# Redone order of the first batch and of the end in a linear-attention kernel, with q's product on VectorE

## The reference

```python
xt = group_norm(x, 32 groups)                    # per batch, then tokens x channels
q, k, v = split(xt @ qkv_w.T + qkv_b)
q = relu(q); k = relu(k + pos_enc)               # 8 heads of 32 channels
z = 1 / (q . k.sum(tokens) + 1e-6)               # one number per token and head
kv = k^T v                                       # 32 x 32 per head
y = x + ((q @ kv) * z) @ proj_w.T + proj_b
```

## Time and profile before

| | |
|---|---|
| median of 3 runs | 2763.82 us (2762.53 to 2765.61) |
| profiled execution | 2772.32 us |
| its span | 2770.5 us |
| PE busy | 2625.4 us, 95% |
| DVE, ACT, POOL busy | 1610.3, 1664.1, 1929.7 us |
| HBM traffic | 519.25 MB read, 119.80 MB written |

### The profile page before, as it was taken

One profiled execution on the slowest core, in us unless ns is written; L12 is line 12 of the kernel. 1 busy time (PEld: TensorE's weight loads), 2 busy tenths in 40 slices (PEclk: granted clock), 3 DMA queues, 4 the chain that ended last, 5 costly groups with the idle time before them and its releaser, 6 DMA issues.

```text
span 2770.5 us, 45261 instructions
## 1 busy us (share of the span) xinstructions
PE 2625.4 (95%) x15812; PEld 2230.1 (80%) x15812; DVE 1610.3 (58%) x2525; ACT 1664.1 (60%) x2544; POOL 1929.7 (70%) x1192
## 2 busy tenths in 40 slices
PE   4779999999999999999999999999999999999985
PEld 3667878888887888878888887888888788888864
DVE  5555656656565566656666565565656566655443
ACT  3556656566565656666666665656656566665632
POOL 2436868687676877868687776867768686876842
PEclk9999999999999999999999999999999999999997
DMA  6446878788787887878788787868868787876756
GB/s 223 141 127 196 271 221 259 227 255 252 226 260 222 267 251 225 262 218 263 228 259 262 228 258 225 267 219 259 259 215 263 227 252 234 257 218 202 220 166 183
DMA packets 357471, 642.07 MB, mean 232 GB/s; under 512 B 34432, under 2 KB 55808, under 8 KB 357248
## 3 DMA queue, kind: packets, MB, share of 16 engines
q1 hardware_dynamic: 357248, 639.18, 74.3%
HBM read 519.25 MB, written 119.80 MB: 231 GB/s over the span
## 4 chain that ended last, share of the span: by engine, by line
PE 72%; DVE 10%; ACT 6%; issue 6%; POOL 3%; DMA 2%; SPq 1%; ACTq 0%; DVEq 0%; POOLq 0%
PE psK L514 17%; PE psX L536 15%; PE psX L567 15%; PE psG L526 10%; PE psG L528 5%; PE psT L505 5%; PE psX L553 3%; ACT xn L961 3%; DVE stats L767 2%; DVE psK L784 2%; DVE kk L789 2%; ACT xt L978 1%; POOL hl L1102 1%; POOL q L1120 1%; DVE zt L839 1%
## 5 line engine op out<-in xcount | busy, mean ns | idle before, releaser
L1116 POOL TENSOR_TENSOR kacc<-kacc,kt 128x512 f32<-128x512 f32 x368 | 478.4, 1300 | 380.5 <-ACT kt L990 378.0
L514 PE MATMUL psK<-wqk,hl 128*128 128x256 f32 x4608 | 651.3, 291 | 16.9 <-POOL hl L1102 16.9
L1102 POOL TENSOR_TENSOR hl<-xn,hl 128x512 fp32r<-128x512 f32 x384 | 497.6, 1318 | 243.2 <-ACT hl L973 243.2
L773 DVE TENSOR_TENSOR xt<-psT,xt 128x512 fp32r<-128x512 f32 x400 | 274.7, 687 | 626.9 <-ACT xt L978 626.8
L526 PE MATMUL psG<-kk,xt 128*128 128x512 f32 x1600 | 588.4, 401 | 21.4 <-DVE kk L789 21.4
L536 PE MATMUL psX<-hl,wqk 128*128 128x512 f32 x2304 | 600.4, 396 | 2.2 <-DVE xr L803 2.2
L514 PEld LDWEIGHTS psK<-wqk,hl 128*128 128x128 f32 x4608 | 580.5, 192 | 22.5 <-POOL hl L1102 22.5
L1120 POOL TENSOR_TENSOR q<-q,zb 128x1024 f32<-128x1024 f32 x192 | 461.5, 2404 | 158.3 <-DMA zb<-z_rows 158.3
L567 PE MATMUL psX<-uhl,mhl 128*128 128x512 f32 (+1 forms) x2364 | 557.7, 385 | 11.7 <-DVE uhl L899 11.7
L983 ACT ACTIVATE kk<-psK 128x512 fp32r<-128x512 f32 x400 | 239.8, 600 | 465.3 <-DVE psK L784 459.9
L567 PEld LDWEIGHTS psX<-uhl,mhl 128*128 128x128 f32 x2364 | 435.2, 189 | 103.0 <-DVE uhl L899 12.5
(11 more groups left out here) (112 smaller groups left out, 2354.8 us busy)
## 6 DMA issues: line engine op xcount, KB each, us to landing
zb<-z_rows SPq DMA_DIRECT2D x768, 128.0 KB, 4.4
posb<-pos_plus_bk SPq DMA_DIRECT2D x375, 256.0 KB, 5.4
xs<-in_x SPq DMA_DIRECT2D x184, 512.0 KB, 5.9
xa<-in_x SPq DMA_DIRECT2D x184, 512.0 KB, 6.0
xr<-in_x SPq DMA_DIRECT2D x184, 512.0 KB, 3.9
y<-xr SPq DMA_DIRECT2D x184, 512.0 KB, 6.7
z_rows<-zt SPq DMA_DIRECT2D x32, 256.0 KB, 5.4
posb<-in_pos SPq DMA_DIRECT2D x25, 256.0 KB, 2.8
```

The costliest lines, as they stand in the source:

```text
L514: last = mm(psK[:, par(n, h), i * C:(i + 1) * C], hl_of(t)[:, a, c, s:s + P], wqk[:, w, c, C:2 * C], start=(j == 0), stop=(j == len(terms) ...
L1102: g.tensor_tensor(hl_of(t)[:, 1, :, s], xn_of(n, t)[:, :, s], hl_of(t)[:, 0, :, s], ALU.subtract).then_inc(xl_ready, 1)
L1116: g.tensor_tensor(both, both, kt[:, par(n, h), :], ALU.add).then_inc(ks_done, 1)
```

## The change

Four things are edited.

1. `scale` moves from POOL to DVE in all steady steps, behind `key_low` of the first half; in step 2 of a batch it stands behind `key_add` of the second half and ahead of `m_low`.
2. The first batch gets its own ACT order (`first_step`), the position addition moves from DVE to POOL (`pos_add`), and the root of the first group norm comes ahead of the copy of the weights.
3. In step `LAST` ACT normalises block 0 of the next batch ahead of `key_high`.
4. The end is rewritten: queries and denominators come ahead of the outputs left over from the batch before (blocks 9 to 12), five places for `zb` instead of two, seven places for u instead of three, two pairs of PSUM banks instead of one for the copies of q, and DVE makes the low part of u ahead of the residual.

```diff
 # DVE, steady step
                 key_low(n, 2 * t)
+                if has_u(n, t) and t != 2:
+                    scale(*u_of(n, t))
...
                     if t == 2 and junction:
+
+                        scale(*u_of(n, t))
                         m_low(n - 1)
                     key_low(n, 2 * t + 1)
+            def scale(n, t):
+                dve.wait_ge(zb_landed[(NBLK * n + t) % 2], zb_no(n, t))
+                v.tensor_tensor(q_of(n, t), q_of(n, t), zb_of(n, t), ALU.mult).then_inc(u_ready, 1)
 # ACT, first batch
+            def first_step(t):
+
+                x_high_t(0, 2 * t)
+                key_high(0, 2 * t)
+                normalise(0, t + 1)
+                x_high_t(0, 2 * t + 1)
+                key_keep(0, 2 * t)
+                xn_high(0, t + 1)
+                if has_q(0, t):
+                    save_q(*q_at(0, t), 0, 2)
+                key_high(0, 2 * t + 1)
+                key_keep(0, 2 * t + 1)
+                if has_q(0, t):
+                    save_q(*q_at(0, t), 1, 0)
 # ACT, steady step
+                if t == LAST and n + 1 < B:
+
+                    normalise(n + 1, 0)
+                    xn_high(n + 1, 0)
                 key_high(n, 2 * t)
 # POOL
             def step(n, t):
-                if has_u(n, t):
-                    scale(*u_of(n, t))
+                if first(n) and t < LAST:
+                    pos_add(2 * t + 2)
+                    xn_low(0, t + 1)
+                    key_sum(0, 2 * t)
+                    if t < LAST - 1:
+                        pos_add(2 * t + 3)
+                    key_sum(0, 2 * t + 1)
+                    return
                 key_sum(n, 2 * t)
+            def scale_last(t):
+                pool.wait_ge(z_last[t % 5], 16 * HPC * (t // 5 + 1))
+                g.tensor_tensor(q_of(B - 1, t), q_of(B - 1, t), z_places[t % 5][:, :, 0:size(t)], ALU.mult).then_inc(u_ready, 1)
 # SP, the end
-            store_y(B - 2, LAST - 2)
-            load_last(4)
-            store_z(B - 1, 0)
-            load_zb(B - 1, 0)
-            load_zb(B - 1, 1)
+            store_z(B - 1, 0)
+            for t in range(5):
+                load_z_last(t)
+            store_y(B - 2, LAST - 3)
+            load_last(4)
+            store_y(B - 2, LAST - 2)
+            store_z(B - 1, 1)
+            load_z_last(5)
...
             for t in range(NBLK):
-                if t + 2 == 8:
-                    store_z(B - 1, 1)
-                if t + 2 < NBLK:
-                    load_zb(B - 1, t + 2)
                 store_last(t)
+                if t + 9 < NBLK:
+                    load_z_last(t + 9)
```

More of the change, by code:

```diff
@@ L91, in build @@
         nbias = sb("nbias", [P, CC])
[L93 to L96, removed]
+        banks8 = ps("banks8", [P, 8, BLK])
+        psG = banks8[:, 0:2, :]
+        psX = banks8[:, 2:5, :]
+        psT = banks8[:, 5, :]
+        psK = banks8[:, 6:8, :]
+        pairs = (psK, banks8[:, 4:6, :])
         zd = nc.dram_tensor("z_rows", (2, P, BLK), F32, kind="Internal").ap()
@@ L105, in build @@
         y_last = [sem(f"y_last{i}") for i in range(8)]
+        z_last = [sem(f"z_last{i}") for i in range(5)]
         x_first = [sem(f"x_first{i}") for i in range(4)]
@@ L421, in step @@
                     next_pos(n, 2 * t + 1)
-                if has_out(n, t):
+                if has_out(n, t) and (n, t) != (B - 1, LAST):
                     store_y(*out_of(n, t))
@@ L558, in output @@
                 k = size(t)
+                mw = mhl_last if n == B - 1 else mhl
                 pe.wait_ge(ul_ready, blk_no(n, t))
@@ L777, in key_add @@
                 s = pos_slot(n, h)
-                dve.wait_ge(pos_landed[s], pos_no(n, h))
                 if first(n):
-                    both = posb[:, s, :].rearrange("p (i n) -> p i n", i=TILES)
-                    v.tensor_tensor(both, both, bk_b[:], ALU.add).then_inc(pos_added, 1)
                     dve.wait_ge(pos_added, h + 1)
+                else:
+                    dve.wait_ge(pos_landed[s], pos_no(n, h))
                 dve.wait_ge(k_done, half_no(n, h))
@@ L992, in save_q, with save_from @@
             def save_q(n, t, m, bank):
+                save_from(n, t, m, psX[:, bank, 0:size(t)])
+            def save_from(n, t, m, src):
                 if m == 0:
-                    wait(act, ul_ready, blk_no(*q_gone(n, t)))
+                    if (n, t) == (B - 1, LAST - 1):
+                        act.wait_ge(kt_ready, NHB * B)
+                    else:
+                        wait(act, ul_ready, blk_no(*q_gone(n, t)))
                 act.wait_ge(q_done, two_no(n, t, m))
-                a(q_of(n, t)[:, m, :], psX[:, bank, 0:size(t)], ACT.Relu, bias=bq[:, m:m + 1]).then_inc(q_saved, 1)
+                a(q_of(n, t)[:, m, :], src, ACT.Relu, bias=bq[:, m:m + 1]).then_inc(q_saved, 1)
             def u_high(n, t, u, used):
@@ L1035, in step @@
                 key_keep(n, 2 * t)
-                nxt = (n, t + 1) if t < LAST else (n + 1, 0)
-                if nxt[0] < B:
-                    normalise(*nxt)
-                    xn_high(*nxt)
+                if (n, t) == (B - 1, LAST):
+                    return
+                if t < LAST:
+                    normalise(n, t + 1)
+                    xn_high(n, t + 1)
                 if t == 2 and not first(n):
@@ new lines, in u_last @@
+                    a(pairs[t % 2][:, :, 0:size(t)], q_of(n - 1, t), ACT.Copy)
+                    if t == 0:
+                        act.wait_ge(q_done, two_no(n - 1, q2, 1))
+                    elif t == 1:
+                        act.wait_ge(q_done, two_no(n - 1, q1, 1))
+                    elif t in (2, 3):
+                        act.wait_ge(g_done, NHB * n)
+                    elif t < 7:
+                        act.wait_ge(o_done, two_no(n - 2, t + 6, 1))
+                    else:
+                        act.wait_ge(o_done, two_no(n - 1, t - 7, 1))
@@ new lines, in u_last @@
+                    a(u_last_of[t % 7][:, 0, :, 0:size(t)], q_of(n - 1, t), ACT.Copy).then_inc(uh_ready, 1)
+                g_copy(n - 1)
+                save_q(n - 1, q2, 1, 0)
+                save_q(n - 1, q1, 0, 2)
+                z_plus(n - 1, 0, psK[:, 0, :])
+                save_from(n - 1, q1, 1, psK[:, 1, :])
+                act.wait_ge(q_done, two_no(n - 1, q0, 1))
+                for m in range(CC):
+                    save_from(n - 1, q0, m, psX[:, 2, m * HALF:(m + 1) * HALF])
@@ L1149, in _ @@
                 scale(B - 2, t)
-                u_low(B - 2, t, uhl)
+            for t, u in ((LAST - 2, hl[:, 0]), (LAST - 1, hl[:, 1]), (LAST, uhl)):
+                u_low(B - 2, t, u)
             for t in range(NBLK):
-                scale(B - 1, t)
+                scale_last(t)
 def kernel(**inputs):
```

167 lines of the change are left out of this document (111 added, 56 removed).

## The result

The changed kernel takes 2673.56 us (median of 4 runs, 2670.30 to 2675.03), the kernel before 2763.18 on the same chip (4 runs, 2760.95 to 2765.61): ratio 0.9674, 95% interval 0.9657 to 0.9691. The forecast was 2681, the range 2652 to 2716. The medians moved by 89.6 us, the forecast said 83.

A forecast was written before the change was run, and what follows sets the result against it. PE was taken as full in the steady part, with loops of waits in the first batch and at the end. Savings of 44 + 6 + 33 = 83 us from 2763.8 gave 2681, range 2652 to 2716.

The forecast's parts named there:

- First batch, -44: First batch: new ACT order and position additions on POOL cut steps from 13.1 to 9.6 us; 44 us less in all.
- Rival A: First batch: POOL or SP sets the pace at 11.5 us per step; 21 saved in place of 44, 2704; chance 0.12.
- The two bounds: First batch: steps of 9.35 us would give 47 less, clock included; steps of 11.5 us would give 17 less.
- Scale on DVE, 0: Steady steps: the scale runs alone on DVE, about 1.2 us, and costs PE 0; up to 3.6 us if meeting POOL.
- Rival D: Steady steps: the scale on DVE meets a POOL operation every step; slower than before, 2795 with 0.6 us waits; chance 0.04.
- Steady part, -6: Batch junctions: 26 us of PE waits recovered, 20 us of new waits in step 2; net 6 us less.
- 1.35 per junction for step 2: Step 2 of each junction: PE waits 0.95 us for the Gram product and 0.4 for step 3's query; 20 us in 15.
- Rival E: Step 2 of each junction: the wait is 3 us, 45 us in place of 20, giving 2706; chance 0.08.
- End, -33: Last batch's end: earlier denominators, then DMA transfers set the finish at 2738 in place of 2770.5; 33 us less.
- the 72 us for 19.1 MB: End: after the first reciprocals land, 36.5 blocks remain to move; 63 us at 302 GB/s, 70 to 75 at 85 to 90%.
- Rival B: End: it stays a loop of waits; 18 us saved in place of 33, giving 2696; chance 0.12.
- C: End: DMAs beat any earlier row and the engines set the end; 54 us saved in place of 33, 2660; chance 0.09.

The follow-up runs named there:

- the run of this part alone: First batch: kernel before with only that batch's edits, 2720.78 us. End: changed kernel with all but the rewritten end put back, 2727.58 us.
- the last version above: Changed kernel with step 2 reordered and, in step LAST, scale ahead of statistics and `key_low`, `xn_low` ahead of `key_sum`: 2652.34 us.
- one order: Changed kernel with the scale on DVE placed behind the residual in every steady step but step 2: 2698.09 us.
- the run with half the broadcast: Changed kernel with only two of the four heads' reciprocals loaded at the end of the last batch: 2663.46 us.
- a reorder of six lines: Changed kernel with step 2 reordered: `key_low` ahead of scale and `m_low` on DVE, `key_high` and `key_keep` ahead of `u_high` on ACT: 2662.17 us.

## Why the prediction was right

- **First batch, -44.** Twelve steps take 144.78 - 29.04 = 115.7 us (117 forecast), the start came 1.85 earlier (1.4), step 12 takes 9.3 (9.5). The traces say -47.1, the run of this part alone -46. The mechanism holds in both halves: adds off DVE, `normalise` out of the loop. Rival A (POOL or SP at 11.5 per step) is out: PE is full in the stretch. The two bounds that I gave were not of one kind: 47 is that of the whole part, 17 that of the twelve steps alone (21 with the rest, as rival A has it); the sum does not rest on it. That step 12 came out at 9.3 is partly luck: 2.61 of it is a wait for `xn_low` that I had not counted, and in the last version above, without this wait, the step takes 6.4.
- **Scale on DVE, 0.** 1.21 us alone (1.2), and PE does not wait for the residual behind it except in step `LAST` (4.7 us in 13 batches), where moving the scale forward took the wait away. Rival D is out for this placing, and its condition is narrower than I wrote: in these runs what costs is not the meeting in a steady step but a meeting ahead of something already late, the root or the next batch's `xn_low`. By the Trainium skill, "SBUF — State Buffer", section "SBUF: two separate sides", the one that starts first keeps the shared port pair for its whole instruction; the 1.91, the 3.50 and the 1.22 us of two-element operations agree with it. It tells the length of the operations, not the price, which was 27 us in one order, while the same meetings in the middle steps left PE no wait in nearly all batches.
- **Steady part, -6.** The mechanism is as forecast, with two errors in size of opposite sign. I had all 26.2 us of waits recovered; 4.7 stay, where the query in step `LAST` waits for the residual. I had 1.35 per junction for step 2; 0.64 + 0.21 = 0.85 was measured, so 11.0 in the 13 junctions of the window and 12.7 in 15, in place of 20. That makes -26.2 + 15.7 = -10.5 in the window of the earlier trace rows, -12.4 by the marks. The medians leave only 5 to 9 for it, and so do the two runs with the old steady part (7 to 10): the profiled run of before was long, 3 to 5 us of it in the steady part. That the net came out near -6 is partly luck, since two errors offset each other. One term is missing from my working: PE's busy time, 3.7 us less at a higher granted clock. Rival E (a wait of 3 us) is out.
- **End, -33.** First denominators 13.7 us after the last transposes (13.4), the store at 17.9 (17.6), the first loads at 20.0 (20.8). The mis-sized term is the 72 us for 19.1 MB. At the measured 295 GB/s they are 65: the share was 0.98, where I had 85 to 90 per cent of the rate. By the marks -40.3 (span), by the run of this part alone -39. Rival B is out. C holds in its first half only: the rate was better than in any row of before (342 GB/s in one stretch of 20 us, 374 in the run with the end alone), but the engines did not set the end yet, as the run with half the broadcast shows.

The sum of 83 was 6.6 too small by the medians: 6 in the end, for its DMA term, and 2 in the first batch, less 1.4 in the steady part.

## What to carry to other kernels

Cost a moved operation by what stands behind it in its new queue: the scale itself was free, and the waits it cost in one step of the batch, 11 us in the list, were two queues' orders; a reorder of six lines gave 8.9 us back. Where two engines take turns, look for the operations that are already late, above all chains of tiny ones; in these runs the rest could meet at almost no price. Split a difference by marks in the trace as well as by the list of waits: the list had 0.28 where the marks had 0.56, and the medians 7.6 where the end itself had 12.2. And take the DMA rate for a stretch that will be full from GB/s divided by share, without a discount, if the loads can be issued ahead: 302 by that rule, 295 measured, in the one stretch that these runs have.

## What the hardware showed that was not expected

The two-element operations of the group norm's root take 0.16 us alone, 0.86 to 2.32 beside a POOL operation, `TENSOR_SCALAR` with one input among them. ACT and DVE operations that read or write PSUM showed no such stretch (`key_low` takes 0.63 to 0.69 us in all 400 places, before and after). The DMA queues moved 342 and 374 GB/s in stretches of 20 us, at shares of 1.06 and 1.05, where 302 to 313 was worked out from the earlier trace rows.
